# Sums of bias and constant vectors made in four groups between the delta chunks, and added to the residual a whole tile at a time

## The chip, the cores and the metric

The kernel runs on one core of a Trainium2 chip. The metric is the device time of one execution in microseconds (us). Before the change the median of three runs is 1797.13 us (1793.7 to 1797.18). The profile comes from a further execution, which took 1801.73 us; its trace spans 1799.9 us, so 1.83 us lie around the span.

PE is TensorE, DVE is VectorE, ACT is ScalarE, POOL is GpSimd, SP is SyncE, which here issues DMAs only. PSUM is the memory that PE writes, SBUF the working memory.

## What is computed

Four layers, each `x = x + attn(norm(x)) + ffn(norm(x))`, over 16 x 256 = 4096 tokens of 128 numbers. Only layer 0 is touched. Its attn is a Mamba block and its ffn a mixture of 16 experts with two chosen per token:

```python
# attn of layer 0
x, res = split(inputs @ W_in);  x = silu(depthwise_conv(x) + b_conv)
delta, B, C = split(inputs @ W_x);  delta = softplus(delta @ W_dt + b_dt)
y = selective_scan(x, delta, A, B, C, D) * silu(res)
attn = y @ W_out + b_out                         # b_out: one vector for all tokens
# ffn of layer 0: expert 0 gives zero, 1 copies the token, 2 and 3 give
# constant vectors, 4..15 are small networks; w are the normalised weights
ffn = sum over the two chosen experts of w * expert_output
```

For each token the sum `b_out + w2 * constant[0] + w3 * constant[1]` has to reach the residual `x`, where w2 and w3 are the weights that the router gave experts 2 and 3 (zero where they were not chosen). The kernel calls this sum `near`.

## The kernel before, in words

Tokens lie in 32 tiles of 128 (`NT`), one token per partition; `g.x` holds the residual as [128, 32, 128]. A program is a list of sections, and a section ends with a clearing of its semaphores and a barrier of all engines (L78). Layer 0 has three: `normalise`, `mamba_front` and `mamba_scan`. The change lies in `mamba_front` alone. Inside a section each engine has its own written order of instructions and waits on semaphores.

In `mamba_front` five strands of work run side by side:

- PE goes through 16 batches of 256 tokens. For each it makes 16 convolution products (L500) and four gate products (L504) into PSUM. Into batches 6 to 11 it weaves the delta chunks of 512 tokens: `chunk(ch)` makes two products, dt (L472) and the rows of B and C (L473), and `steps(ch)` expands dt by `w_dt` (L483). Before batch 7 stands `steps(0)`, then `chunk(1)`; before batch 8 `steps(1)`, then `chunk(2)`, and so on to `steps(4)` before batch 11. `steps(ch)` waits for `dtx_done` of its chunk, and `chunk(ch)` for `dtx_done` and `bc_done` of the chunk ahead of it. Three more chunks follow the last batch.
- ACT takes the batches out of PSUM with SiLU (L542 for the gate, L544 for `u`; each batch counts `act_done` up by one), takes the absolute value of each delta chunk (L520), and after the last batch makes exponentials (L524) and logarithms (L529).
- DVE first runs the routing (the choice of experts, its places and weights, up to L1240), then `make_near`: 32 instructions for the first constant (`b_out + w2 * constant[0]`, L590), a wait for all of them, and 32 for the second. Only then come `take(0)`, which copies dt and B/C out of PSUM (L572, L573), `give(ch)`, which adds `b_dt` to delta (L578), and so on in the order give, take, give, take. At the end `finish(ch)` (L585) combines delta with the logarithm, eight instructions of 128x1024.
- POOL issues indirect DMAs that scatter the normalised tokens to the experts' buffer (`scatter_choice`, L1049), 56 of the 64 here and eight in the scan section. Scatter n waits for `act_done` of batch min(16, 3 + n//4). Behind each scatter stands `add_near(n)`, which adds half a tile (64 columns) of `near` to `g.x` (L447). The first half of a tile waits until DVE has made its second constant. Ahead of scatter 32 POOL waits until the first 32 have landed and rewrites the token numbers (L1041). After scatter 55 eight half tiles are left.
- SP stores gate, B/C rows and copies of the normalised rows, in an order written out by hand.

The next section, `mamba_scan`, begins on POOL with L768 and L771; ACT and DVE wait for what POOL makes there.

Of the kernel before, what the change touches and what calls it, by code (L numbers as in the profile page):

```python
# [9 lines left out]
ALU = mybir.AluOpType  # L10
# [4 lines left out]
D = 128  # L15
BATCH, T = 16, 256
N = BATCH * T
NT = N // P
# [48 lines left out]
@contextmanager  # L67
def section(nc, title, *names):


    sems = [nc.alloc_semaphore(f"{title}_{n}") for n in names]
    with ExitStack() as ctx:
        def sb(name, shape, dt=F32):
            return ctx.enter_context(nc.sbuf_tensor(f"{title}_{name}", shape, dt))

        yield namedtuple("Section", names + ("sems", "sb"))(*sems, sems, sb)
    nc.clear_and_free_semaphores(sems)
    nc.all_engine_barrier()  # L78
# [283 lines left out]
def mamba_front(nc, g, t, u, gate_d, delta, bc_d, r, disp, ybuf, scattered, f):  # L362
# [5 lines left out]
    NCH = N // CH  # L368
    W = 2 * DS
    FROM, BESIDE = 6, 5  # L370
    with section(nc, "front", *ROUTE, "xz_ready", "gate_ready", "gate_out0", "gate_out1", "act_done", "biased",
                 "marked", "const_made", "b_out_in", "rows_set", "delta_in", "dt_ready", "dtx_done", "z_ready", "zb_done", "bc_done",
                 "bc_out0", "bc_out1", "abs_done", "exp_done", "ln_done", "delta_done", "neg_a") as s:
# [3 lines left out]
        near = s.sb("near", [P, NT, D])  # L377
# [13 lines left out]
        def dt_bank(ch):  # L391
            return 0 if ch == BESIDE + 1 else 6

        def bc_bank(ch):
            return 1 if ch == BESIDE + 1 else 7

        def z_bank(ch):
            return 2 if ch == BESIDE + 1 else 4
# [4 lines left out]
        def cols(ch):  # L403
            return slice(ch * CH, (ch + 1) * CH)

        with nc.Block() as block:

            @block.sync
            def _(sp):
                for dst, src in ((w_dt_in, "m_w_dt_in"), (w_bc, "m_w_bc"), (w_dt, "m_w_dt"), (b_dt, "m_b_dt")):  # L410
                    sp.dma_start(dst[:], t[src]).then_inc(s.delta_in, 16)
                sp.dma_start(b_out[:], t["m_b_out"].to_broadcast([P, D])).then_inc(s.b_out_in, 16)
                for dst, src in ((f.a_neg, "m_a_log"), (f.d_col, "m_d"), (f.w_out, "m_w_out")):
                    sp.dma_start(dst[:], t[src]).then_inc(f.scan_in, 16)
                sp.dma_start(consts[:], t["f0_const"].to_broadcast([P, 2, D])).then_inc(s.b_out_in, 16)
                for k in range(2):
                    sp.dma_start(ybuf[k * N:(k + 1) * N, :].rearrange("(t p) d -> p t d", p=P),
                                 g.xn[:]).then_inc(s.rows_set, 16)

                def store_rows(ch):  # L420
                    sp.wait_ge(s.bc_done, ch + 1)
                    sp.dma_start(bc_d[0, :, cols(ch)], bc[:, ch % 2]).then_inc(bc_out[ch % 2], 16)

                for b in range(BATCH):
                    sp.wait_ge(s.gate_ready, b + 1)
                    sp.dma_start(gate_d[:, :, b * T:(b + 1) * T], gate[:, b % 2]).then_inc(gate_out[b % 2], 16)
                    if 0 <= b - FROM - 1 < BESIDE:
                        store_rows(b - FROM - 1)
                for ch in range(BESIDE, NCH):
                    store_rows(ch)  # L430
                for p in range(2):
                    sp.wait_ge(gate_out[p], BATCH // 2 * 16)
                    sp.wait_ge(bc_out[p], NCH // 2 * 16)
                sp.wait_ge(s.rows_set, 32)

            @block.gpsimd
            def _(pool):
                job.gpsimd(pool)
                mark_choice(nc, g, s.marked, 0)
                pool.wait_ge(s.marked, 1)  # L440
                pool.wait_ge(s.r_placed, 1)
                def add_near(n):
                    i, half = divmod(n, 2)
                    to = slice(half * D // 2, (half + 1) * D // 2)
                    if half == 0:
                        pool.wait_ge(s.const_made, NT + i + 1)
                    nc.gpsimd.tensor_tensor(g.x[:, i, to], g.x[:, i, to], near[:, i, to], ALU.add).then_inc(s.biased, 1)  # L447

                for n in range(2 * SCATTERED_IN_FRONT):
                    if n == NT:  # L450
                        pool.wait_ge(scattered, NT * 16)
                        mark_choice(nc, g, s.marked, 1)
                        pool.wait_ge(s.marked, 2)
                    pool.wait_ge(s.act_done, min(BATCH, 3 + n // 4))
                    scatter_choice(nc, pool, scattered, disp, g, r, n)
                    add_near(n)
                for n in range(2 * SCATTERED_IN_FRONT, 2 * NT):
                    add_near(n)

            @block.tensor  # L460
            def _(pe):
# [102 lines left out]
            @block.vector  # L564
            def _(dve):

                def take(ch):
                    dve.wait_ge(s.dt_ready, ch + 1)
                    if ch >= 2:
                        dve.wait_ge(s.z_ready, ch - 1)  # L570
                        dve.wait_ge(bc_out[ch % 2], ch // 2 * 16)
                    nc.vector.tensor_copy(dtx[:, ch % 2], g.ps[:, dt_bank(ch), :]).then_inc(s.dtx_done, 1)  # L572
                    nc.vector.tensor_copy(bc[:, ch % 2], g.ps[0:W, bc_bank(ch), :]).then_inc(s.bc_done, 1)  # L573

                def give(ch):
                    dve.wait_ge(s.z_ready, ch + 1)
                    for c in range(DC):
                        ins = nc.vector.tensor_scalar(delta[:, c, cols(ch)], g.ps[:, z_bank(ch) + c, :], b_dt[:, c:c + 1],  # L578
                                                      None, ALU.add)
                    ins.then_inc(s.zb_done, 1)  # L580

                def finish(ch):
                    dve.wait_ge(s.ln_done, ch + 1)
                    d = delta[:, :, cols(ch)]
                    nc.vector.scalar_tensor_tensor(out=d, in0=d, scalar=0.0, in1=e[:, :, cols(ch)],  # L585
                                                   op0=ALU.max, op1=ALU.add).then_inc(s.delta_done, 1)

                def make_near(j, tiles):
                    for i in tiles:
                        nc.vector.scalar_tensor_tensor(out=near[:, i, :], in0=consts[:, j, :], scalar=r.const_w[:, j, i:i + 1],  # L590
                                                       in1=near[:, i, :] if j else b_out[:], op0=ALU.mult,
                                                       op1=ALU.add).then_inc(s.const_made, 1)

                job.vector(dve)
                dve.wait_ge(s.b_out_in, 32)
                for j in range(2):
                    if j:
                        dve.wait_ge(s.const_made, NT)
                    make_near(j, range(NT))
                dve.wait_ge(s.delta_in, 64)  # L600
                take(0)
                for ch in range(1, BESIDE):
                    give(ch - 1)
                    take(ch)
                give(BESIDE - 1)
                take(BESIDE)
                take(BESIDE + 1)
                give(BESIDE)
                give(BESIDE + 1)
                take(BESIDE + 2)  # L610
                finish(0)
                finish(1)
                give(BESIDE + 2)
                for ch in range(2, NCH - 1):
                    finish(ch)
                dve.wait_ge(s.neg_a, 1)
                nc.vector.tensor_scalar(f.a_neg[:], f.a_neg[:], -1.0, None, ALU.mult).then_inc(s.neg_a, 1)
                finish(NCH - 1)
# [403 lines left out]
SCATTERED_IN_FRONT = 28  # L1022
# [15 lines left out]
def mark_choice(nc, g, marked, k):  # L1038


    nc.gpsimd.iota(g.xn_row[:, :, ID].bitcast(I32), pattern=[[P, NT]], base=k * N, channel_multiplier=1,  # L1041
                   allow_small_or_imprecise_dtypes=True).then_inc(marked, 1)


def scatter_choice(nc, pool, done, disp, g, r, n):


    k, i = divmod(n, NT)
    pool.indirect_dma_start(disp, bass.IndirectOffsetOnAxis(ap=r.scat_i[:, k, i:i + 1], axis=0), g.xn_row[:, i, :], None,  # L1049
                            bounds_check=disp.shape[0] - 1, oob_is_err=False).then_inc(done, 16)  # L1050
# [1999 lines left out]
```

## Time and profile before

| what | before |
|---|---|
| median of three runs | 1797.13 us |
| profiled execution, its span | 1801.73 us, 1799.9 us |
| busy: PE, DVE, ACT, POOL (share of the span) | 83%, 71%, 52%, 46% |
| mean granted TensorE clock (1 is full speed, 2.4 GHz) | 0.927 |
| `mamba_front`, first instruction to POOL's last | 40.13 to 172.08 us |
| first instruction of `mamba_scan` | 177.61 us |

A timeline row reads: start in us, duration in us, engine, line, operation, what is written <- what is read, shapes, count; in brackets the idle time of the engine before the row and what ended it. A row with x32 is a merged run of 32 instructions. A wait row reads: who waited, at which line, for whom; total us, times, longest us.

### The profile page before, as it was taken

The page shows a single profiled execution, that of the slowest core. Times are in us where ns is not written, and L with a number is a line of the kernel's source. Part 1 is how long each engine was busy: PE and PEld are TensorE (multiplying, and loading weights), DVE is VectorE, ACT ScalarE, POOL GpSimd, SP SyncE. Part 2 cuts the span into 40 slices and gives each one's busy share as a digit, 9 for nine tenths or more (in the row PEclk, how much of TensorE's full clock was granted, in tenths as well). Part 3 has the DMA queues.
Part 4 walks back from the last instruction along what each step waited for, and adds up shares of the span by engine and source line. Part 5 has one row for each costly group of instructions (what it writes and reads, how often), then busy time and mean ns, then how long its engine had stood idle before and what let it go on. Part 6 is the DMA issues. An engine that isn't in the chain of part 4 may idle for free. (4 is left out here: it accounts for less than half of the span.)

```text
span 1799.9 us, 32108 instructions
## 1 busy us (share of the span) xinstructions
PE 1490.2 (83%) x11190; PEld 917.6 (51%) x11190; DVE 1274.0 (71%) x2266; ACT 943.5 (52%) x1777; POOL 819.8 (46%) x882
## 2 busy tenths in 40 slices
PE   5794688888877777569799999955889999878997
PEld 5562144444432226246577776631345444466886
DVE  7823899999999997767445467758743799565335
ACT  1225377777756742435444456635644677533442
POOL 1288888888886761568144443222400000046341
PEclk9997899999999997779899999976899999879999
DMA  4521986766757653665422236307531242221223
GB/s 144 150 65 46 201 177 177 189 189 177 175 152 208 172 147 128 210 174 108 63 60 56 57 71 102 49 10 190 81 60 52 37 71 41 73 93 53 76 82 100
DMA packets 193566, 200.95 MB, mean 112 GB/s; under 512 B 22474, under 2 KB 142569, under 8 KB 193152
## 3 DMA queue, kind: packets, MB, share of 16 engines
q1 hardware_dynamic: 181816, 177.33, 40.2%
q0 software_dynamic: 11520, 21.52, 4.4%
q8 instruction: 93, 1.52, 0.4%
q14 instruction: 65, 0.53, 0.1%
q10 hardware_dynamic: 72, 0.03, 0.0%
HBM read 144.45 MB, written 57.48 MB: 112 GB/s over the span
## 5 line engine op out<-in xcount | busy, mean ns | idle before, releaser
L792 POOL TENSOR_TENSOR xn_t<-scan_b_rows,scan_du 128x512 f32<-128x512 f32 x256 | 325.9, 1291 | 87.8 <-DMA scan_b_rows<-states 44.6
L816 PE MATMUL banks<-scan_hc,ident 128*128 128x512 f32 x512 | 279.6, 633 | 83.9 <-DVE scan_hc L991 83.0
L984 DVE TENSOR_TENSOR_SCAN banks<-banks,xn_t 128x512 f32<-128x512 f32 x256 | 312.7, 1222 | 22.2 <-POOL xn_t L792 19.0
L2462 ACT ACTIVATE att_pr<-banks 128x768 f32<-128x768 f32 (+1 forms) x256 | 234.3, 917 | 124.7 <-PE banks L2354 72.6
L816 PEld LDWEIGHTS banks<-scan_hc,ident 128*128 128x128 f32 x512 | 82.6, 192 | 228.4 <-DVE scan_hc L991 208.2
L918 ACT ACTIVATE banks<-delta,scan_exp_centre,a_neg 128x510 f32<-128x510 f32 x256 | 198.6, 776 | 0.3
L991 DVE TENSOR_TENSOR scan_hc<-banks,scan_c_rows 128x512 f32<-128x512 f32 x256 | 177.0, 691 | 8.8
L2507 DVE TENSOR_REDUCE att_mb<-banks 128x4 f32<-128x1024 f32 x128 | 153.8, 1221 | 20.4 <-PE banks L2321 15.5
L2370 PE MATMUL banks<-att_pr,att_vx 128*32 128x256 f32 (+1 forms) x2048 | 153.6, 373 | 5.0 <-ACT att_ot L2467 3.7
L2503 DVE TENSOR_REDUCE att_mb<-banks 128x6 f32<-128x768 f32 x128 | 121.5, 956 | 45.0 <-PE banks L2328 44.0
L2321 PE MATMUL banks<-att_ks,att_qs 48*128 48x256 bf16 (+1 forms) x1024 | 110.8, 274 | 41.6 <-DMA att_ks<-k_parts 36.6
L1614 POOL IOTA xn_tok<- 128x32 int32 x1 | 0.2, 188 | 305.9 <-POOLq L78 305.9
L1430 POOL DMA_INDIRECT ybuf<-att_yo,att_xin x72 | 69.8, 970 | 125.6 <-DVE att_yo L1414 123.3
L2346 PE MATMUL banks<-att_qs,att_ks 50*128 50x256 bf16 (+1 forms) x1024 | 107.8, 267 | 15.2 <-DMA att_qs<-att_mt 12.4
L917 ACT COPY banks<-zeros 128x2 f32<-128x2 f32 x256 | 40.7, 159 | 150.1 <-DVE scan_hc L991 139.4
L1330 PE MATMUL banks<-grouped_w,att_xt 128*128 x288 | 99.0, 467 | 0.5 <-DVE att_xt L1396 0.3
L1379 ACT ACTIVATE att_a<-banks 128x352 f32<-128x352 f32 x72 | 33.4, 464 | 106.4 <-PE banks L1330 106.4
L1049 POOL DMA_INDIRECT disp<-xn_tok,places x64 | 67.9, 1062 | 35.8 <-ACT u L544 24.1
L2286 POOL DMA_INDIRECT disp<-xn_tok,places x64 | 65.6, 1025 | 33.5 <-issue 12.9
L2321 PEld LDWEIGHTS banks<-att_ks,att_qs 48*128 48x128 bf16 x1024 | 48.3, 98 | 59.0 <-issue 26.0
L2346 PEld LDWEIGHTS banks<-att_qs,att_ks 50*128 50x128 bf16 x1024 | 39.7, 94 | 70.2 <-issue 39.5
L1631 POOL DMA_INDIRECT ybuf<-gau_eyo,gau_exin x40 | 40.3, 1008 | 74.4 <-DVE gau_eyo L1925 66.7
(389 smaller groups left out, 3170.5 us busy)
## 6 DMA issues: line engine op xcount, KB each, us to landing
scan_b_rows<-states SPq DMA_DIRECT2D x128, 256.0 KB, 5.2
scan_c_rows<-states SPq DMA_DIRECT2D x128, 256.0 KB, 4.3
scan_ew<-f_packed SPq DMA_DIRECT2D x12, 578.0 KB, 5.4
q_parts<-att_p_parts SPq DMA_DIRECT2D x16, 384.0 KB, 3.9
k_parts<-att_p_parts SPq DMA_DIRECT2D x16, 384.0 KB, 5.9
att_qs<-q_parts SPq DMA_DIRECT2D x64, 96.0 KB
att_ks<-k_parts SPq DMA_DIRECT2D x64, 96.0 KB
disp<-blank_rows SPq DMA_DIRECT2D x1, 4680.0 KB, 15.2
```

The costliest lines, as they stand in the source:

```text
L792: nc.gpsimd.tensor_tensor(bu[:, i % AHEAD], b_rows[:, q % HELD], du[:, b % 2, c], ALU.mult).then_inc(s.bu_made, 1)
L816: nc.tensor.matmul(g.ps[:, Y_BANK[c], :], g.ident[:], hc[:, i % RING], start=False, stop=(q % DS == DS - 1)).then_inc(s.sum_done, 1)
L918: nc.scalar.activation(inner(g.ps[:, DA + i % RING, :]), inner(delta[:, c, span(b)]), ACT.Exp, scale=a_neg[:, c, n:n + 1], bias=exp_centre ...
L984: v.tensor_tensor_scan(states, states, bu[:, i % AHEAD], 0.0, ALU.mult, ALU.add).then_inc(s.scan_done, 1)
L991: v.tensor_tensor(hc[:, i % RING], states, c_rows[:, q % HELD], ALU.mult).then_inc(s.hc_ready, 1)
L1330: ins = nc.tensor.matmul(g.ps[:, 4 * p + 1 + m, 0:H1], xt[:, p, :], rows(w13[:, bass.ds(expert[j], 1), m * H1:(m + 1) * H1]), start=True, ...
L2321: ins = nc.tensor.matmul(g.ps[:, 2 * m_slot(i) + half, lo:hi], qs[rows_of, p, j, q * P:(q + 1) * P], ks[rows_of, p, j, 0:hi - lo], start=T ...
L2346: ins = nc.tensor.matmul(g.ps[:, 2 * s_slot(i) + half, k * T:k * T + T - q0], ks[rows_of, p, j, k * P:(k + 1) * P], qs[rows_of, p, j, q0:T ...
L2370: ins = nc.tensor.matmul(g.ps[r * 32:(r + 1) * 32, O_BANK, q0:T], vx[:, b % 2, k, 4 * jg + r, :], pr[:, i % RING, half, k * T:k * T + T - q0],
L2462: nc.scalar.activation(pr[:, i % RING], g.ps[:, at:at + 2, 0:W], ACT.Exp, scale=scale).then_inc(s.p_ready, 1)
L2503: v.tensor_reduce(mb[:, b % 2, j, :].rearrange("p (g n) -> p g n", g=2), g.ps[:, at:at + 2, 0:W].rearrange("p g (n k) -> p g n k", k=P), A ...
L2507: v.tensor_reduce(mb[:, b % 2, j, :], g.ps[:, at:at + 2, :].rearrange("p g (n k) -> p (g n) k", k=T), AX_X, ALU.max).then_inc(s.m_taken, 1)
```

## The change

DVE makes `near` in four groups of eight tiles. A group is eight instructions for the first constant, a wait for these eight, and eight for the second. Group 0 stands where all of `make_near` stood, ahead of `take(0)`; groups 1, 2 and 3 stand behind `take(1)`, `take(2)` and `take(3)`. POOL adds a whole tile (128 columns) at a time, behind every odd scatter from n = 9 on, so 24 tiles inside the scatter loop and eight behind it. Each add waits for the tile's second constant: `const_made` counts 16 per group. The first eight scatters have no add behind them. Nothing else is moved.

```diff
--- before.py
+++ after.py
@@ -368,6 +368,7 @@
     NCH = N // CH
     W = 2 * DS
     FROM, BESIDE = 6, 5
+    GROUP, LAG = 8, 8
     with section(nc, "front", *ROUTE, "xz_ready", "gate_ready", "gate_out0", "gate_out1", "act_done", "biased",
                  "marked", "const_made", "b_out_in", "rows_set", "delta_in", "dt_ready", "dtx_done", "z_ready", "zb_done", "bc_done",
                  "bc_out0", "bc_out1", "abs_done", "exp_done", "ln_done", "delta_done", "neg_a") as s:
@@ -439,13 +440,11 @@
                 mark_choice(nc, g, s.marked, 0)
                 pool.wait_ge(s.marked, 1)
                 pool.wait_ge(s.r_placed, 1)
-                def add_near(n):
-                    i, half = divmod(n, 2)
-                    to = slice(half * D // 2, (half + 1) * D // 2)
-                    if half == 0:
-                        pool.wait_ge(s.const_made, NT + i + 1)
-                    nc.gpsimd.tensor_tensor(g.x[:, i, to], g.x[:, i, to], near[:, i, to], ALU.add).then_inc(s.biased, 1)
-
+                def add_near(i):
+                    pool.wait_ge(s.const_made, i // GROUP * 2 * GROUP + GROUP + i % GROUP + 1)
+                    nc.gpsimd.tensor_tensor(g.x[:, i, :], g.x[:, i, :], near[:, i, :], ALU.add).then_inc(s.biased, 1)
+
+                added = 0
                 for n in range(2 * SCATTERED_IN_FRONT):
                     if n == NT:
                         pool.wait_ge(scattered, NT * 16)
@@ -453,9 +452,11 @@
                         pool.wait_ge(s.marked, 2)
                     pool.wait_ge(s.act_done, min(BATCH, 3 + n // 4))
                     scatter_choice(nc, pool, scattered, disp, g, r, n)
-                    add_near(n)
-                for n in range(2 * SCATTERED_IN_FRONT, 2 * NT):
-                    add_near(n)
+                    if n >= LAG and n % 2:
+                        add_near(added)
+                        added += 1
+                for i in range(added, NT):
+                    add_near(i)
 
             @block.tensor
             def _(pe):
@@ -593,15 +594,20 @@
 
                 job.vector(dve)
                 dve.wait_ge(s.b_out_in, 32)
-                for j in range(2):
-                    if j:
-                        dve.wait_ge(s.const_made, NT)
-                    make_near(j, range(NT))
+                def make_group(k):
+                    tiles = range(k * GROUP, (k + 1) * GROUP)
+                    make_near(0, tiles)
+                    dve.wait_ge(s.const_made, (2 * k + 1) * GROUP)
+                    make_near(1, tiles)
+
+                make_group(0)
                 dve.wait_ge(s.delta_in, 64)
                 take(0)
                 for ch in range(1, BESIDE):
                     give(ch - 1)
                     take(ch)
+                    if ch < NT // GROUP:
+                        make_group(ch)
                 give(BESIDE - 1)
                 take(BESIDE)
                 take(BESIDE + 1)
```

## Rows read from the trace of the kernel before

**Rows 1.** Waits of all engines, 38 to 185 us.
```profile
core 0 of [0], span 1799.9 us
...
DVE banks L984 <- POOL xn_t L792: 14.5, 1, 14.5
...
POOL scan_exp_centre L768 <- POOLq L78: 5.5, 1, 5.5
```

**Rows 2.** Timeline of DVE.
```profile
67.29 8.49 DVE L590 SCALAR_TENSOR_TENSOR front_near<-front_consts,const_w,front_b_out 128x128 f32<-128x128 f32 x32 [0.16 <-DVE w L1240]
75.82 9.63 DVE L590 SCALAR_TENSOR_TENSOR front_near<-front_consts,const_w,front_near 128x128 f32<-128x128 f32 x32
85.38 0.68 DVE L572 COPY front_dtx<-banks 128x512 f32<-128x512 f32 x1
...
100.69 0.69 DVE L572 COPY front_dtx<-banks 128x512 f32<-128x512 f32 x1 [0.42 <-PE banks L473]
...
114.96 1.41 DVE L578 TENSOR_SCALAR delta<-banks,front_b_dt 128x512 f32<-128x512 f32 x2 [4.52 <-PE banks L483]
...
155.07 2.34 DVE L585 SCALAR_TENSOR_TENSOR delta<-delta,front_e 128x1024 f32<-128x1024 f32 x2
...
161.37 1.22 DVE L585 SCALAR_TENSOR_TENSOR delta<-delta,front_e 128x1024 f32<-128x1024 f32 x1 [0.38 <-ACT front_e L529]
...
167.46 1.21 DVE L585 SCALAR_TENSOR_TENSOR delta<-delta,front_e 128x1024 f32<-128x1024 f32 x1
```

**Rows 3.** Timeline of PE.
```profile
72.35 1.05 PE L473 MATMUL banks<-xn_t,front_w_bc 128*32 128x512 f32 x2
...
76.87 1.03 PE L504 MATMUL banks<-xn_t,w_in_sb 128*128 128x256 f32 x4
86.11 3.78 PE L483 MATMUL banks<-front_dtx,front_w_dt 128*128 128x512 f32 x4 [8.21 <-DVE front_dtx L572]
...
96.94 1.88 PE L483 MATMUL banks<-front_dtx,front_w_dt 128*128 128x512 f32 x4
...
104.99 1.88 PE L483 MATMUL banks<-front_dtx,front_w_dt 128*128 128x512 f32 x4
```

**Rows 4.** Windows, all engines: stretch, its length, busy by engine, granted clock, DMA.
```profile
86.00:97.00 11.00, 10.89 (x29) 5.98 (x30) 3.33 (x6) 1.06 (x1) 9.63 (x15) 0.74 0.11 34
97.00:145.00 48.00, 48.00 (x191) 34.88 (x189) 9.47 (x14) 15.33 (x29) 40.66 (x62) 1.00 0.24 74
```

**Rows 5.** Timeline of POOL, front section.
```profile
64.72 1.15 POOL L1049 DMA_INDIRECT disp<-xn_tok,places  x1 [24.05 <-ACT u L544]
...
76.97 0.99 POOL L1049 DMA_INDIRECT disp<-xn_tok,places  x1 [0.36 <-issue]
...
78.48 0.99 POOL L1049 DMA_INDIRECT disp<-xn_tok,places  x1 [0.17 <-issue]
...
123.42 0.34 POOL L447 TENSOR_TENSOR x_tok<-x_tok,front_near 128x64 f32<-128x64 f32 x1
...
125.88 0.99 POOL L1049 DMA_INDIRECT disp<-xn_tok,places  x1 [0.78 <-POOL xn_tok L1041]
...
154.67 3.61 POOL L1049 DMA_INDIRECT disp<-xn_tok,places  x1 [0.17 <-issue]
158.30 2.86 POOL L447 TENSOR_TENSOR x_tok<-x_tok,front_near 128x64 f32<-128x64 f32 x1
161.33 0.99 POOL L1049 DMA_INDIRECT disp<-xn_tok,places  x1 [0.16 <-issue]
...
169.56 2.52 POOL L447 TENSOR_TENSOR x_tok<-x_tok,front_near 128x64 f32<-128x64 f32 x9
```

**Rows 6.** One line of the last layer: POOL's adds of 128x128, ns min/median/max.
```profile
L1624 POOL TENSOR_TENSOR x_tok<-x_tok,xn_tok x32: 437/479/665, 1601.6 to 1653.6; 128x128 f32<-128x128 f32 x32
```

**Rows 7.** Timeline of POOL, scan section: second of two scatters in a row.
```profile
185.70 0.97 POOL L1049 DMA_INDIRECT disp<-xn_tok,places  x1 [0.30 <-issue]
```

**Rows 8.** Windows of L590 alone: stretch, length, DVE busy (count), clock, DMA.
```profile
76.30:85.50 9.20, 9.15 (x31) 0.78 0.17 54
```

**Rows 9.** Timeline of ACT: `u` of batch 11, `act_done` 12.
```profile
127.81 0.83 ACT L544 ACTIVATE u<-banks,b_conv 128x256 f32<-128x256 f32 x2
```

## The prediction

> **What bounds the kernel now.** The chain of waits on the page starts in the last layer and says nothing of layer 0, so I read forward from the changed place. The list of waits came first, to see who waits for the end of the front section: behind it DVE stands 14.5 us until POOL has made the scan's first product, and POOL itself needs 5.5 us from its last front instruction to its first one in the scan [rows 1]. So the question is which engine ends the front last. On POOL's timeline that is its last run of adds, over at 169.56 + 2.52 = 172.08; DVE is done at 167.46 + 1.21 = 168.67 [rows 5, 2]. POOL sets the end, by 3.4 us.
>
> Next I asked why each of the two is so late. DVE makes all 64 instructions of `near` in one piece, from 67.29 to 85.4, and only then copies the first delta chunk, at 85.38 [rows 2]. Two engines stand meanwhile. PE had that chunk's products ready at 72.35 + 1.05 = 73.40 and ran out of work at 86.11 - 8.21 = 77.90; it waits 8.21 us for the copy [rows 3]. When it goes on, its granted clock is 0.74 on average from 86 to 97, against 1.00 from 97 to 145, where it is busy for all 48.00 of 48 us [rows 4]. POOL issues its first scatter at 64.72 and the second at 76.97, for behind the first stands an add that needs a finished tile of `near`; after that it is never idle for long: a scatter and a half add every 1.51 us [rows 5]. So both strands start late because of the same 18 us of DVE, and neither catches up before the section ends.
>
> **The change part by part.** *DVE's block is split.* Ahead of `take(0)` stand 8 + 8 instructions. At 8.49/32 = 0.265 us and 9.63/32 = 0.30 us [rows 2] they take 4.5 us, so DVE reaches `take(0)` at 71.8. It waits for the products until 73.40 and has copied dt by 74.1. PE asks for it at 77.90, so 3.8 us of cover are left and the 8.21 us go entirely.
>
> *PE.* From 77.90 it runs at the full-speed rhythm: from one `steps` to the next 104.99 - 96.94 = 8.05 us, where the first round after the stall took 96.94 - 86.11 = 10.83 us, 2.8 more, at the low clock [rows 3, 4]. The second `steps` thus comes at 77.90 + 8.05 = 85.95 instead of 96.94. All of PE, ACT and DVE behind it moves by 11.0 us, since each of them is paced by PE there. That puts DVE's end at 168.67 - 11.0 = 157.7.
>
> *Three groups between the chunks.* They are not free by themselves; what hides them is the idle time of DVE between `take(ch)` and `give(ch)`, of which the smallest of the three is 4.52 us [rows 2]. A group is 16 instructions. Nothing else on DVE or POOL beside it: 16 x 0.265 = 4.2 us. Beside a busy POOL: 31 of them took 9.15 us [rows 8], 0.295 each, so 4.7 us; I take this, since POOL runs all the while. It overruns the smallest gap by 0.2 us. That reaches nobody: the copy that PE needs at 104.99 was done at 100.69 + 0.69 = 101.38 [rows 2, 3], so 3.6 us more are free. Queued behind a group are `give` and the next `take`; ACT waits for the one, PE for the other, and both have this slack. A group costs PE nothing until it exceeds 4.5 + 3.6 = 8.1 us.
>
> *POOL's scatters come earlier.* Scatter 0 ends at 64.72 + 1.15 = 65.87. Seven more follow without an add, each 0.99 plus the 0.30 between two scatters in a row [rows 7], so scatter 8 starts at 65.87 + 0.30 + 7 x 1.29 = 75.2. From there 24 pairs: 0.99 + 0.30 + 0.99, an add of a whole tile, and the 0.17 that follows an add [rows 5]. No 128x128 add of this line is in the trace, but the last layer has 32 of the same form: 0.437 at least, 0.479 in the median [rows 6]; I take 0.45, with 0.02 in front. The pair is 2.92 us (two scatters with two half adds were 3.02), all pairs 70.1 us. Rewriting the token numbers costs what it cost: 125.88 - 123.76 - 0.17 = 1.95 us. Eight adds of 0.45 are left, 3.6 us. Unhindered, POOL would end at 75.2 + 70.1 + 1.95 + 3.6 = 150.8. Below, the add is at least a half add, 2.52/9 = 0.28 [rows 5], and the gap 0.17: together 8.5 us less, by which DVE would decide. Above, 0.479 and 0.36 us [rows 6, 5]: 2.4 us more. The new waits on `const_made` hold nobody: scatter 25, with the first tile of group 1, comes at some 100 us, and group 1 lies ahead of `give(1)`, which follows PE's 85.95 + 1.88 = 87.8.
>
> *The waits on ACT.* Each scatter also waits for a batch of ACT, which limits how early POOL can be. Batch 11 ended at 127.81 + 0.83 = 128.64 [rows 9], so now at 117.6; scatter 36, which needs it, is due at 75.2 + 14 x 2.92 + 1.95 = 118.0. It fits, barely. A faster POOL would gain little.
>
> *The tail.* DVE's `finish` instructions hold POOL up. Beside two of them a scatter took 3.61 instead of 0.99 us and an add 2.86 instead of 0.34; a scatter that began at 161.33, just ahead of one at 161.37, was not held [rows 5, 2]. Summed: unhindered, POOL would have ended at 125.88 + 24 x 1.51 + 8 x 0.28 = 164.4, and it ended at 172.08, so it lost 7.7 us to eight instructions of 2.34/2 = 1.17 us, 9.4 in all. They move with DVE to 144.1, when POOL still has 6.8 us of work (before: 9.3). I charge the same 7.7, so POOL ends at 158.5. The bounds: no loss, and DVE's end at 157.7 decides; or all 9.4 us, 160.2, with the dearer pairs 162.6.
>
> The Trainium skill, "SBUF — State Buffer", section "Who interferes with whom", says that a VectorE instruction with two SBUF inputs blocks a GpSimd instruction that reads SBUF, and infers that it leaves descriptor generation alone. The held add agrees; the scatter of 3.61 us speaks against the second half, the one at 161.33 for it.
>
> **Sum.** The front ends at 158.5 instead of 172.08: 13.5 us less. The barrier's 5.5 us and all that follows are the same instructions in the same relations, so I charge nothing there. From the profiled execution this gives 1801.73 - 13.5 = 1788.2; that execution lies 4.6 us above the median of the runs, and against the median it gives 1797.13 - 13.5 = 1783.6.
>
> **Rivals.** (1) *POOL loses less in the tail*: `finish` holds its adds but not its scatters, POOL is done ahead of DVE, and DVE's 157.7 ends the front: 14.4 us less, 1782.7. For it: the scatter at 161.33. Against: the one of 3.61. It is where the skill's inference about descriptor generation would lead.
> (2) *POOL's strand is dearer*: 162.6, only 9.5 us less, 1787.6. For it: the new order of scatter, scatter, whole add beside DVE's groups is shown nowhere as such. Against: beside 31 of the same DVE instructions scatters kept 0.99 us [rows 5, 8].
> (3) *PE does not win back the clock*: only the 8.2 us of the stall are saved, DVE ends at 160.5, POOL about 161.5: 10.6 less, 1786.5. Against: without the idle stretch nothing in the rows lowers it.
> (4) *No effect*: what is won in the front is lost again in the scan, where the same transfers and the last eight scatters come earlier beside other traffic: 1797. Against: the scan's start waits for POOL's first products [rows 1] and nothing there is tied to the time.
> (5) *Slower*: DVE's groups and POOL's adds read the same memory and hold each other up. If each of the 16 instructions waits out a whole scatter, 0.87 us instead of 0.295, a group is 14 us; beyond 8.1 each microsecond stops PE, three times 5.9, and each stop costs 2.8 more at the low clock: 26 us against 13.5 saved, 1810. It decides from a group of 9.8 us on. For it: `finish` and POOL do collide, and the 0.03 us that an instruction lost [rows 8, 2]. Against: those same 0.03 are all that 31 of them lost beside POOL.
>
> **How the numbers follow.** The forecast has 0.55, (1) 0.14, (2) 0.16, (3) 0.03, (4) 0.07, (5) 0.05. What a measurement of this kernel can tell from no change is about 0.2%, 3.6 us; the first four lie beyond it: faster 0.88, same 0.07, slower 0.05. The range reaches from the best case at the lowest run shown (1793.7 - 14.4 = 1779.3) to the dearest POOL strand (1787.6) with 2 us for the spread of runs and a part of what lies between it and no effect: 1779 to 1790.
>
> **What would show it.** PE's idle time ahead of its first L483 gone, and that row near 77.9 with 1.88 us; granted clock 1.00 from 78 to 134; DVE's idle time ahead of `give` of chunks 1 to 3 filled by rows of 16 L590s of about 4.7 us, and `take(2)` to `take(4)` still 8.05 us apart; POOL's second scatter near 66.2, its ninth near 75.2, its last add near 158.5, DVE's last L585 ending near 157.7; the scan's first row at about 164. I am wrong if PE shows new idle time ahead of an L483, if POOL's pairs exceed 3.1 us, or if the scan grows by what the front lost.

## The result, and the profile after

| | before | after |
|---|---|---|
| median, 8 runs each | 1795.74 us | 1784.45 us |
| ratio to before, 95% interval | | 0.9934, 0.9915 to 0.9953 |
| profiled execution | 1801.73 us | 1783.17 us |
| front's first row to scan's first row | 137.46 us | 125.57 us |

The changed kernel is faster by 11.3 us in the medians and by 11.9 in the ratio (0.0066 x 1795.74). Forecast were 13.5 us, a time of 1783.6 and a range of 1779 to 1790: the time lies in it, 0.85 us above the number. Two single executions are left out of the times and ratios of the experiments below: 2387 us in e4 and 2775 us in e5.

The two profiled executions differ by 18.5 us, more than the medians do. To see what of that belongs to the change, mark the same instruction in both: POOL's first row of the front, of the scan, of layer 1 and of layer 3 (timeline rows: start, duration, engine, line). Before:

```profile
40.15 0.15 POOL L1244 IOTA route_rev<- 128x16 f32 x1 [24.51 <-POOLq L78]
...
177.61 0.10 POOL L768 MEMSET scan_exp_centre<- 128x1 f32 x1 [5.54 <-POOLq L78]
...
696.22 0.15 POOL L1244 IOTA norm_rev<- 128x9 f32 x1 [19.69 <-POOLq L78]
...
1587.14 0.15 POOL L1244 IOTA gau_rev<- 128x8 f32 x1
```

And after:

```profile
40.40 0.15 POOL L1250 IOTA route_rev<- 128x16 f32 x1 [24.51 <-POOLq L78]
...
165.97 0.10 POOL L774 MEMSET scan_exp_centre<- 128x1 f32 x1 [5.85 <-POOLq L78]
...
684.48 0.15 POOL L1250 IOTA norm_rev<- 128x9 f32 x1 [19.72 <-POOLq L78]
...
1570.17 0.15 POOL L1250 IOTA gau_rev<- 128x8 f32 x1
```

The front lost 11.9 us (137.46 to 125.57), the scan up to layer 1 took 518.6 and 518.5, and the stretch to layer 3 took 890.9 and 885.7. I don't put the last 5.2 us down to the change: layers 1 and 2 are untouched, and in the changed kernel profiled once more and in the variants below that stretch took anything from 881.6 to 888.1. There is only one profile of the kernel before, so this is argued and not shown. The front's 11.9 us agrees with the medians, and nothing of it was handed back in the scan.

PE after, on its timeline, where [rows 3] stood:

```profile
72.60 1.04 PE L474 MATMUL banks<-xn_t,front_w_bc 128*32 128x512 f32 x2
...
77.12 1.03 PE L505 MATMUL banks<-xn_t,w_in_sb 128*128 128x256 f32 x4
77.98 1.88 PE L484 MATMUL banks<-front_dtx,front_w_dt 128*128 128x512 f32 x4
...
86.03 1.88 PE L484 MATMUL banks<-front_dtx,front_w_dt 128*128 128x512 f32 x4
```

The bracket with 8.21 us is gone, and the first L484 takes 1.88 us instead of 3.78. The window of all engines answers to [rows 4] (stretch, length, busy by engine, granted clock): PE is busy throughout at full clock.

```profile
78.00:134.00 56.00, 56.00 (x219) 39.91 (x217) 27.13 (x66) 17.62 (x33) 45.15 (x55) 1.00 0.23 73
```

DVE after, where [rows 2] stood:

```profile
69.86 2.22 DVE L591 SCALAR_TENSOR_TENSOR front_near<-front_consts,const_w,front_near 128x128 f32<-128x128 f32 x8
73.75 0.69 DVE L573 COPY front_dtx<-banks 128x512 f32<-128x512 f32 x1 [1.68 <-PE banks L474]
...
82.94 2.60 DVE L591 SCALAR_TENSOR_TENSOR front_near<-front_consts,const_w,front_b_out 128x128 f32<-128x128 f32 x8
85.57 2.69 DVE L591 SCALAR_TENSOR_TENSOR front_near<-front_consts,const_w,front_near 128x128 f32<-128x128 f32 x8
88.19 1.39 DVE L579 TENSOR_SCALAR delta<-banks,front_b_dt 128x512 f32<-128x512 f32 x2
...
153.30 1.23 DVE L586 SCALAR_TENSOR_TENSOR delta<-delta,front_e 128x1024 f32<-128x1024 f32 x1 [1.45 <-ACT front_e L530]
155.19 4.62 DVE L586 SCALAR_TENSOR_TENSOR delta<-delta,front_e 128x1024 f32<-128x1024 f32 x1 [0.67 <-ACT front_e L530]
...
160.08 1.21 DVE L586 SCALAR_TENSOR_TENSOR delta<-delta,front_e 128x1024 f32<-128x1024 f32 x1
```

DVE now waits for PE ahead of the first copy, 1.68 us, where PE waited for DVE. Group 1 takes 5.3 us and fills the idle time ahead of `give` without reaching PE. And one `finish` near the end takes 4.62 us instead of 1.2: that was not forecast.

POOL after, where [rows 5] stood:

```profile
65.03 1.15 POOL L1055 DMA_INDIRECT disp<-xn_tok,places  x1 [24.12 <-ACT u L545]
66.50 0.97 POOL L1055 DMA_INDIRECT disp<-xn_tok,places  x1 [0.31 <-issue]
...
75.56 0.97 POOL L1055 DMA_INDIRECT disp<-xn_tok,places  x1 [0.30 <-issue]
...
92.12 1.63 POOL L1055 DMA_INDIRECT disp<-xn_tok,places  x1 [0.30 <-issue]
...
144.02 3.36 POOL L1055 DMA_INDIRECT disp<-xn_tok,places  x1 [0.17 <-issue]
147.68 3.26 POOL L1055 DMA_INDIRECT disp<-xn_tok,places  x1 [0.30 <-issue]
150.95 1.22 POOL L445 TENSOR_TENSOR x_tok<-x_tok,front_near 128x128 f32<-128x128 f32 x1
...
155.39 4.73 POOL L445 TENSOR_TENSOR x_tok<-x_tok,front_near 128x128 f32<-128x128 f32 x9
```

The second scatter comes at 66.50 instead of 76.97, the ninth at 75.56. Beside `finish` scatters take over 3 us, and the nine adds at the end, 155.39 to 160.12, lie over the long `finish` (155.19 to 159.81). One by one, the first eight of them start 0.41 us apart and take 0.44 to 0.47 us each; the ninth starts at 158.69 and takes 1.43. So the `finish` waited out eight adds, and the ninth add waited for it. The scan's first row follows POOL's last add by 5.85 us and DVE's last instruction (161.29) by 4.68.

### The profile page after: what moved, and what is told of

Read it like the earlier page. It is cut to its first block and busy times, and to the rows that moved or that the text cites. A ratio compares the mean times of both kernels' runs of the same rounds, so it can differ in the third digit from the quotient of the medians.

```text
span 1781.4 us, 32076 instructions
## 1 busy us (share of the span) xinstructions
PE 1488.6 (84%) x11190; PEld 918.4 (52%) x11190; DVE 1277.8 (72%) x2266; ACT 943.2 (53%) x1777; POOL 812.7 (46%) x850
## 3 DMA queue, kind: packets, MB, share of 16 engines
q1 hardware_dynamic: 181816, 177.33, 40.4%
## 5 line engine op out<-in xcount | busy, mean ns | idle before, releaser
L1055 POOL DMA_INDIRECT disp<-xn_tok,places x64 | 70.1, 1096 | 40.2 <-ACT u L545 25.4
L1402 DVE COPY att_xt<-banks 128x128 f32<-128x128 f32 x72 | 20.9, 292 | 75.3 <-PE banks L1326 75.3
```

## The experiments

All are compared with the kernel before. "Front" is the time from the front's first row to the scan's first row, as above. e0, e1, e2 and e4 ran on one chip, e3, e5, e6 and e7 on another, each beside the kernel before. The fronts of e2, e5 and e6 began at 37.3 to 37.5 us, the others at 40.2 to 40.7, so the ends of these three in the fourth column are to be read some 3 us later. T, R and P are theories that the expectations state (P at e3).

| kernel | ratio to before (95%) | front, us | last of POOL, of DVE | scan's first row behind them |
|---|---|---|---|---|
| before | | 137.46 | 172.08, 168.67 | 5.53, 8.94 |
| e0, the change again | 0.9946 (0.9923 to 0.9968) | 125.55 | 160.43, 161.59 | 5.85, 4.69 |
| e1, groups only | 0.9972 (0.9955 to 0.9988) | 135.38 | 170.18, 157.67 | 5.54, 18.05 |
| e2, POOL's part only | 0.9988 (0.9967 to 1.0009) | 135.67 | 167.35, 168.52 | 5.85, 4.68 |
| e3, last adds behind `finish` | 0.9931 (0.9909 to 0.9952) | 126.44 | 161.22, 157.81 | 5.54, 8.95 |
| e4, DVE makes the adds | 0.9890 (0.9858 to 0.9921) | 118.12 | 144.15, 157.70 | 14.44, 0.89 |
| e5, as e4, POOL waits for DVE | 0.9926 (0.9899 to 0.9953) | 122.92 | 141.09, 154.63 | 19.22, 5.68 |
| e6, DVE makes the last 8 adds | 0.9892 (0.9862 to 0.9923) | 121.90 | 153.68, 154.85 | 5.54, 4.37 |
| e7, as e4 | 0.9876 (0.9845 to 0.9906) | 119.84 | 146.15, 159.66 | 14.41, 0.90 |

**e0: the changed kernel again.** No edit.

> The changed kernel again, on the chip of the experiments below. Theory T (the tail): the front's end moved by 11 to 12 us, less than the 13.5 forecast, because POOL's nine adds in a row held DVE's next-to-last `finish` for 4.62 instead of 1.22 us and so put the front's end on DVE's last one; the scan's first row comes at about 166, the time is 11 to 13 us below the kernel before, and such a long `finish` row shows again near 155. Rival R (pacing): that long row is a chance of one execution, and the front's end is set by PE and ACT alone; then the row is 1.2 us here and the scan still begins at about 166.

The long `finish` is there again, 4.60 us beside nine adds of 4.72 us in a row, so it is no chance of one execution. Whether it costs anything this run can't say. The time, 9.7 us below the kernel before by the ratio and 6.8 by the medians, is less than T's 11 to 13.

**e1: DVE's groups alone.** POOL's half adds stay, one behind every scatter (the body of `add_near` and the last loop are not shown):

```diff
-                def add_near(i):
...
+                def add_near(n):
...
-                    if n >= LAG and n % 2:
-                        add_near(added)
-                        added += 1
+                    add_near(n)
```

> DVE's four groups alone; POOL adds half a tile behind every scatter, as before. Both theories: PE's stall of 8.21 us is gone and PE runs at the full clock from 78 on. T: POOL's second scatter waits for the first finished tile at about 70, 6 us earlier than before, so POOL still has some 14 us of work when DVE's `finish` begins at 144, loses 8 to 9 us to it and ends the front at 165 to 168: 4 to 7 us faster than before. R: the front ends with DVE at about 158 to 161, and the gain is that of the whole change, 11 us or more.

The front is 2.1 us shorter and DVE is done at 157.67, 12.5 us ahead of POOL. POOL decides, as T said, and the rival's 11 us are out. (By the ratio the time is 5.0 us lower, but the front gave only 2.1 of it.) T had POOL end at 165 to 168 and it ends at 170.18. One reason is that each group holds up an add of POOL's for over a microsecond: on POOL's timeline

```profile
83.70 1.24 POOL L448 TENSOR_TENSOR x_tok<-x_tok,front_near 128x64 f32<-128x64 f32 x1
...
92.47 1.18 POOL L448 TENSOR_TENSOR x_tok<-x_tok,front_near 128x64 f32<-128x64 f32 x1
...
99.37 1.67 POOL L448 TENSOR_TENSOR x_tok<-x_tok,front_near 128x64 f32<-128x64 f32 x1
...
167.66 2.52 POOL L448 TENSOR_TENSOR x_tok<-x_tok,front_near 128x64 f32<-128x64 f32 x9
```

where nearly all other half adds ahead of `finish` take 0.34; these three cost 3.1 us. The other is that the second scatter came at 72.07, only 4.9 us earlier than before, since DVE reached `near` later in this execution (68.69 against 67.29).

**e2: POOL's part alone.** DVE makes all of `near` ahead of the first chunk (`add_near`'s wait, which follows suit, and the body of `make_group` are not shown):

```diff
...
-                make_group(0)
+                for j in range(2):
+                    if j:
+                        dve.wait_ge(s.const_made, NT)
+                    make_near(j, range(NT))
...
-                    if ch < NT // GROUP:
-                        make_group(ch)
```

> POOL's part alone: whole tiles behind every second scatter; DVE makes all of `near` ahead of the first delta chunk, as before. Both theories: PE's stall of 8.2 us stays. T: POOL, paced by ACT's batches from scatter 20 on, is done at about 155, just as `finish` begins, so the front ends with DVE at 168.7 instead of POOL's 172.1: 3 to 4 us faster than before. The two parts alone then give 8 to 10 us, the whole 12. R: if POOL's early start were what brings the gain, 9 us or more.

The front is 1.8 us shorter, less than the 3 to 4 of T and far from R's 9; the time can't be told from no change. POOL's early start is eaten up at once: beside each of DVE's two runs of 32 instructions (65.46 to 73.95 and 73.99 to 82.48) one scatter is held until 0.8 us behind the run's end, while others pass in 1.0 to 1.1 us. Timeline of POOL:

```profile
66.96 1.01 POOL L1050 DMA_INDIRECT disp<-xn_tok,places  x1 [0.30 <-issue]
68.27 6.52 POOL L1050 DMA_INDIRECT disp<-xn_tok,places  x1 [0.31 <-issue]
75.10 1.14 POOL L1050 DMA_INDIRECT disp<-xn_tok,places  x1 [0.30 <-issue]
76.54 6.78 POOL L1050 DMA_INDIRECT disp<-xn_tok,places  x1 [0.30 <-issue]
```

So POOL ended at 167.35, which stands for 170 in a front that begins at 40.2, and not at 155. The parts alone take 2.1 and 1.8 us off the front, the whole 11.9. In both POOL still ends the front. e1 frees PE and DVE but keeps POOL waiting for the first finished tile. e2 starts POOL's scatters early, but DVE's long runs hold them until at the ninth scatter nothing is left of the lead (84.91, which stands for 87.5, against 87.57 before), and PE still stands 7.85 us, so `finish` comes late. Only where the groups shorten DVE's runs does POOL's early start count.

**e4 and e7: DVE makes all adds,** in its idle stretch between the fifth `give` and the sixth `take`; POOL only scatters (the removed lines of its adds are not shown):

```diff
...
+                dve.wait_ge(s.const_made, 2 * NT)
+                for k in range(NT // 4):
+                    to = slice(4 * k, 4 * k + 4)
+                    nc.vector.tensor_tensor(rows(g.x[:, to, :]), rows(g.x[:, to, :]), rows(near[:, to, :]),
+                                            ALU.add).then_inc(s.biased, 1)
                 take(BESIDE)
```

> The changed kernel, but the 32 adds go to DVE: eight instructions of 128x512 in its idle stretch of 22 us behind the fifth `give`; POOL only scatters. T: nothing of POOL's is left when `finish` begins at 144 (its last scatter, paced by ACT's batch 16, ends at 140 to 143), all `finish` rows are 1.2 us, DVE ends the front at about 158 and the scan's first row comes at about 163, 3 us earlier than in the changed kernel: about 15 us below the kernel before. R: the scan's first row stays at about 166 and the time at that of the changed kernel.

> DVE makes all 32 adds, again, on the chip of these runs. P and T: scan's first row at 158.6, 7.4 us ahead of the changed kernel's 165.97 (its front began at 40.4, as here); against the kernel before 18 to 20 us.

It beats both kernels: 0.9890 and 0.9876. The eight adds cost DVE 4.89 us of 22 idle ones, all `finish` rows are 1.2 us, and DVE ends at 157.70 as T said. But the scan's first row comes at 158.59, not at 163. Rows of e4, DVE and then POOL:

```profile
113.50 4.89 DVE L605 TENSOR_TENSOR x_tok<-x_tok,front_near 128x512 f32<-128x512 f32 x8
...
156.48 1.22 DVE L576 SCALAR_TENSOR_TENSOR delta<-delta,front_e 128x1024 f32<-128x1024 f32 x1
```

```profile
158.59 0.10 POOL L769 MEMSET scan_exp_centre<- 128x1 f32 x1 [14.44 <-POOLq L78]
```

T was too pessimistic by the 4.4 us that it still charged for leaving the section, which here take 0.89. That told me that T had the wrong end of it: perhaps the 5.5 us behind POOL's last instruction are POOL's own, and the long `finish` costs nothing. e3, e5 and e6 were to decide that. (e7's front is 1.7 us longer than e4's, lost on PE before the first chunk ended. Its time is 22 us below the kernel before, more than the 18 to 20 expected and than the 17.6 of its front; what lies behind the front there no experiment explains.)

**e3: the last adds behind `finish`.**

```diff
+                pool.wait_ge(s.delta_done, NCH)
                 for i in range(added, NT):
                     add_near(i)
```

> The changed kernel, but POOL's eight left-over adds wait until DVE's last `finish` is done, so that neither can hold the other. Times as from a front that begins at 40.4. Theory P (POOL's leaving): behind its last instruction POOL needs 5.5 to 5.9 us until the scan's first row, DVE behind its own only about 0.9, so POOL's last instruction sets the front's end and DVE's long `finish` of 4.62 us costs next to nothing. Then all `finish` rows are 1.2 to 1.4 us, DVE ends at about 157.7, the adds at 161.4, and the scan's first row comes at about 167, 1 us later than in the changed kernel. Theory T (the long `finish` set the end): the scan's first row comes 1 us behind the last add, at about 162.4, 3.5 us earlier.

P's numbers came out within 0.3 us. DVE, then POOL:

```profile
155.10 1.23 DVE L587 SCALAR_TENSOR_TENSOR delta<-delta,front_e 128x1024 f32<-128x1024 f32 x1 [0.67 <-ACT front_e L531]
...
156.60 1.21 DVE L587 SCALAR_TENSOR_TENSOR delta<-delta,front_e 128x1024 f32<-128x1024 f32 x1
```

```profile
155.29 1.35 POOL L445 TENSOR_TENSOR x_tok<-x_tok,front_near 128x128 f32<-128x128 f32 x1
157.89 3.33 POOL L445 TENSOR_TENSOR x_tok<-x_tok,front_near 128x128 f32<-128x128 f32 x8 [1.25 <-DVE delta L587]
166.76 0.10 POOL L775 MEMSET scan_exp_centre<- 128x1 f32 x1 [5.54 <-POOLq L78]
```

With the adds out of its way the `finish` that took 4.62 us takes 1.23, so it was the run of adds that held it. DVE is done 3.5 us earlier, and the front is 0.9 us longer all the same. T is refuted: DVE's long `finish` did not set the end.

**e5: POOL, without work, waits for DVE.** As e4, and one wait at the end of POOL's program:

```diff
                     scatter_choice(nc, pool, scattered, disp, g, r, n)
+                pool.wait_ge(s.delta_done, NCH)
```

> DVE makes the 32 adds, and POOL, which is done at 144, waits for DVE's last `finish` before it leaves the section: one wait more, no work. P: POOL's leaving, hidden in the run without this wait, comes behind DVE's end at 157.7 again, and the scan's first row at 162 to 163 instead of 158.6: 4 us slower than without the wait. T: nothing waits for a POOL that has nothing to do; the row stays at 158.6.

The scan's first row comes at 160.31, which stands for 163.3 in a front that begins at 40.4: P said 162 to 163, T 158.6. One wait makes the front 4.8 us longer than e4's, and 3.1 longer than e7's with its late first chunk. The time, 1782.4 us against e7's 1773.5 on the same chip, differs by more than the front; most of the rest lies between layers 1 and 3 (888.1 against 881.6 us), and no experiment explains it. What POOL does there, the view of the section's first line (L407, where the section ends) shows: a DRAIN of POOL's queue (duration min/median/max in ns, start of first and last).

```profile
L407 POOLq DRAIN  x1: 4642/4642/4642, 154.8 to 154.8; - x1
```

It starts 0.2 us behind DVE's last instruction and takes 4.64 us although POOL's last scatter was over 13.7 us ago; no DMA packet moves meanwhile. In e4 the same view has

```profile
L407 POOLq DRAIN  x1: 11645/11645/11645, 137.2 to 137.2; - x1
```

from 137.2, issued behind the queued scatters, to 148.8, which is 4.7 us behind the last of them at 144.15 and 8.9 us ahead of DVE's end: hidden. The kernel before, and then the changed one, show the same price at the front's end:

```profile
L406 POOLq DRAIN  x1: 12432/12432/12432, 164.3 to 164.3; - x1
```

```profile
L407 POOLq DRAIN  x1: 13833/13833/13833, 151.0 to 151.0; - x1
...
L407 DVEq DRAIN  x1: 5065/5065/5065, 156.3 to 156.3; - x1
```

POOL's DRAIN ends at 176.7 and at 164.8, each 4.7 us behind POOL's last add. DVE's own DRAIN ends with its last instruction (161.4 in the changed kernel).

**e6: only the eight left-over adds go to DVE** (the same lines as in e4, for tiles 24 to 31, and POOL's last loop removed).

> The changed kernel with only its eight left-over adds moved to DVE, two instructions of 128x512 in the idle stretch behind the fifth `give`. The 24 adds between the scatters stay with POOL. P: no `finish` is held over 1.4 us, DVE ends at 157.7, POOL's last add ends at 155.9, and with its 5.5 us the scan's first row comes at 161.4 to 161.8: 4 us below the changed kernel, some 16 below the kernel before. T: DVE's end decides, the row comes at 158.6, as where DVE makes all adds.

```profile
152.35 1.33 POOL L445 TENSOR_TENSOR x_tok<-x_tok,front_near 128x128 f32<-128x128 f32 x1
159.22 0.10 POOL L777 MEMSET scan_exp_centre<- 128x1 f32 x1 [5.54 <-POOLq L78]
```

P again: 5.54 us behind POOL's last add. This front began at 37.32 instead of 40.40, so P's 161.4 to 161.8 stand for 158.3 to 158.7 here, and T's 158.6 for 155.5; 159.22 is P's, 0.5 late.

## Why the prediction was right, point by point

- *What bounds the front.* Right: POOL sets its end, before and after. Behind its last instruction come 5.5 us; e5 shows 4.64 of them to be POOL's DRAIN. I charged the 5.5 us as "the barrier's" and as a constant. That held, to 0.3 us, only because POOL's last instruction plus 5.5 us stayed later than DVE's plus the 0.89 of e4, even in the change, where DVE's came 1.2 us behind POOL's. So POOL's lead over DVE was not 3.4 us but some 8 (172.08 + 5.53 against 168.67 + 0.89), and the cases in which DVE decides, my lower bound and rival (1) with 14.4 us, were priced too low: in e4 DVE decides, and the front is 19.3 us shorter.
- *The 8.21 us of PE go entirely, and 2.8 more with the clock.* Right to 0.1 us: the first L484 at 77.98 with 1.88, the second 8.05 later; 86.03 against 96.94 is 10.9 for 11.0. Granted clock 1.00 from 78 to 134.
- *Three groups hidden in DVE's idle time.* Right for PE, which never waited. Their price was 4.8 to 5.4 us instead of 4.7 (4.4 in e4, beside scatters alone), and they weren't free for POOL, which I had not charged: from the ninth scatter (75.56) to the 53rd (144.02) POOL took 68.5 us where 22 pairs and the 1.95 make 66.2. This term of 2.3 us is the largest mis-sized step upward. 1.7 us of it lie in the seven pairs beside the groups, which took 3.00 to 3.66 us instead of 2.92, three of them above the 3.1 that I had named as a sign of being wrong; most of the rest is 0.35 us more for rewriting the token numbers. Rival (2), a dearer strand of POOL's, had the direction right and 4.1 us for it. Rival (5) named the collision, but a group stayed far below its 14 us, and what DVE lost reached nobody, while POOL's loss reached the front's end. Rival (3) is out: the clock came back.
- *POOL's early scatters.* Right: the second at 66.50 (forecast 66.2), the ninth at 75.56 (75.2); an add 0.47 instead of 0.45; the waits on ACT held nobody for long.
- *The tail.* From 144.02 POOL needed 16.1 us; 9.4 of work and 7.7 of loss were forecast. It lost 1.0 us less: eight of its last nine adds ran undisturbed while the `finish` waited for them, and only the ninth was held. Rival (1) is out: scatters were held, 3.36 and 3.26 us, and the front didn't end with DVE.
- *Sum.* POOL's last add was forecast at 158.5, 158.75 with this execution's later start (0.25), and came at 160.12: 0.1 + 2.3 - 1.0 = 1.4 us late. The last 0.3 us lie in the 5.85 behind it instead of 5.5. So 11.9 in place of 13.5. What the 0.3 are stays open; they show in the three runs with the held `finish` (the change, e0, e2) and in no other, and lie behind the end of POOL's DRAIN.
- *The time.* It came out closer than the gain, 0.85 us off where the gain was 1.6 to 2.2 us short, because the kernel before took 1795.74 us in the eight runs and not the 1797.13 that I had subtracted from. That part is luck.
- *Nothing given back in the scan.* Right: 518.6 and 518.5 us; in the variants 517.9 to 519.5. Rival (4) is out.

On the page that the prediction cites, "SBUF — State Buffer" of the Trainium skill: its section "SBUF: two separate sides" says that whichever of the two instructions starts first has the shared port pair "for the whole instruction". Single adds agree: in e3 an add that starts 0.2 us behind a `finish` takes 1.35 us and the `finish` 1.23. Runs do not: in the change the `finish` also starts 0.2 us ahead of the first add, and yet waits for eight adds, 4.62 us; and in e2 a scatter waits for most of a run of 32 DVE instructions of 0.27, 6.78 us. The inference in section "Who interferes with whom", made there for `tensor_tensor` with both inputs in SBUF, that descriptor generation is left alone, has these held scatters against it, unless what waits in them is the reading of `places`, which lies in SBUF; the rows can't tell the two apart. That the engines wait for this port, and not for something else that they share, no run shows.

## What to carry to other kernels

Before you price a faster strand, list every strand's last instruction in the stage and what each engine still needs to leave it: here POOL's leaving costs 5.5 us when POOL is last and nothing when POOL is done 13.5 us ahead of DVE (e4), and so a version that moved POOL's adds to DVE's idle stretch made the front 17.6 to 19.3 us shorter instead of 11.9. Two edits of which each needs the other show next to nothing alone (2.1 and 1.8 us here), so judge them together. A run of short instructions on DVE or POOL can hold the other engine for most of the run and not for one instruction (4.62 us beside nine adds, 6.5 and 6.8 us beside 32 instructions of DVE's): put such runs where the other one has nothing due.

## What the runs showed of the hardware that I had not expected

- POOL's DRAIN at the section's end takes 4.64 us with nothing left to do (e5); in the stretch from 172.1 to 177.5 of the kernel before there is no DMA packet and no work on any engine. What it does in that time the trace doesn't show. It is no fixed price of a section's end: in the kernel before, POOL's DRAIN takes 0.03 to 0.05 us in the setup and in the four sections of L157, in which POOL issues no indirect DMA. It ends 4.7 us behind POOL's last instruction in the scan, which has 56 of them, but 1.5 us behind it in layer 1's section (L2208), which has 136. What sets its length stays open.
- Who holds whom between DVE and POOL is not settled by who starts first. A `finish` that starts 0.2 us ahead of POOL's add took 1.23 us where one add stood there (e3, and 1.22 in e6) and 4.62 where nine did (the change). Adds took up to 2.9 us beside `finish` rows that were not held (before, e1). Before, 31 of DVE's instructions ran beside POOL's scatters with scatters at 0.99 [rows 5, 8]; in e2 the same lines held two scatters for 6.5 and 6.8 us. What decides it stays open.
